# Experts: routing weights spread over partitions by DMA, expert weights laid out by the host, a quarter of the tokens routed first

## What is computed

```python
logits = x @ gate_w.T;  scores = sigmoid(logits);  sc = scores + e_bias
group_scores = top_k(sc.reshape(T, 8, 4), 2)[0].sum(-1)
masked = where(group in top_k(group_scores, 4), sc, 0)
topk_idx = top_k(masked, 6)[1];  topk_w = scores at topk_idx, normed, * 2.5
combine = zeros(T, 32) with topk_w at topk_idx
h = relu(einsum('th,eih->tei', x, up_w)) ** 2 * combine[:, :, None]
out = einsum('tei,ehi->th', h, down_w) + relu(x @ shared_up_w.T) ** 2 @ shared_down_w.T
```

## Time and profile before

| what | us |
|---|---|
| median of 3 runs (3858.93 to 3862.2) | 3859.53 |
| the profiled execution | 3866.06 |
| its span, first to last instruction | 3864.3 |
| PE busy in the span | 3442.3 (89%) |
| DVE busy | 2871.3 (74%) |
| ACT busy | 2329.9 (60%) |
| POOL busy | 1067.8 (28%) |

### The profile page before, as it was taken

One profiled execution on the slowest core, in us unless ns is written; L12 is line 12 of the kernel. 1 busy time (PEld: TensorE's weight loads), 2 busy tenths in 40 slices (PEclk: granted clock), 3 DMA queues, 4 the chain that ended last, 5 costly groups with the idle time before them and its releaser, 6 DMA issues. The chain is left out here.

```text
span 3864.3 us, 97882 instructions
## 1 busy us (share of the span) xinstructions
PE 3442.3 (89%) x39003; PEld 1703.8 (44%) x39003; DVE 2871.3 (74%) x3920; ACT 2329.9 (60%) x4575; POOL 1067.8 (28%) x1874
## 2 busy tenths in 40 slices
PE   5885999999999999984999582999999999999988
PEld 3442444444444444433666581444444444444435
DVE  5776788888888888854344896888888888888852
ACT  3663677777777777771332530777777777777663
POOL 4552223222222322201665002232222223222201
PEclk9997999999999999996999795999999999999998
DMA  3332222232222223201000002222322222232200
GB/s 98 75 79 58 61 55 60 55 77 61 56 63 54 59 58 75 57 12 25 1 0 1 0 0 61 53 60 56 76 63 54 63 54 59 62 70 63 49 16 22
DMA packets 165138, 194.88 MB, mean 50 GB/s; under 512 B 32166, under 2 KB 124123, under 8 KB 164715
## 3 DMA queue, kind: packets, MB, share of 16 engines
q1 hardware_dynamic: 164714, 189.03, 20.8%
HBM read 27.88 MB, written 2.10 MB: 8 GB/s over the span
## 5 line engine op out<-in xcount | busy, mean ns | idle before, releaser
L586 ACT ACTIVATE cross_Pr<-cross_sT 128x512 f32<-128x512 f32 (+1 forms) x3584 | 1833.6, 563 | 768.8 <-PE cross_sT L508 767.8
L649 DVE TENSOR_REDUCE cross_nm<-cross_ring 128x2 f32<-128x802 f32 x2048 | 1975.6, 991 | 323.7 <-PE cross_ring L474 295.3
L508 PE MATMUL cross_sT<-cross_Q,cross_K 64*128 64x256 bf16 x13312 | 1044.2, 273 | 49.3 <-ACT cross_Pr L586 42.2
L527 PE MATMUL cross_oT<-cross_Pr,cross_V 128*9 128x256 f32 x13312 | 1029.8, 381 | 0.0
L508 PEld LDWEIGHTS cross_sT<-cross_Q,cross_K 64*128 64x128 bf16 x13312 | 511.1, 95 | 771.8 <-ACT cross_Pr L586 637.1
L474 PE MATMUL cross_ring<-cross_K,cross_Q 64*128 64x401 bf16 x4096 | 662.3, 337 | 62.2 <-DMA cross_K<-cross_kparts 33.5
L401 POOL TENSOR_TENSOR cross_mp<-cross_nm,cross_one 128x8 bf16<-128x8 f32 x128 | 25.9, 202 | 1373.6 <-DVE cross_nm L654 1373.6
L527 PEld LDWEIGHTS cross_oT<-cross_Pr,cross_V 128*9 128x9 f32 x13312 | 197.6, 88 | 412.6 <-issue 245.1
L474 PEld LDWEIGHTS cross_ring<-cross_K,cross_Q 64*128 64x128 bf16 x4096 | 199.0, 94 | 202.7 <-DVE cross_nm L649 106.9
L1104 DVE TENSOR_TENSOR moe_rc<-moe_r,moe_bank 128x512 f32<-128x512 f32 x128 | 87.9, 687 | 170.8 <-ACT moe_r L995 170.8
L876 POOL TENSOR_TENSOR moe_hh<-moe_r,moe_rc 128x512 f32<-128x512 f32 x128 | 162.5, 1270 | 160.0 <-DVE moe_rc L1104 159.3
(11 more groups left out here) (296 smaller groups left out, 3035.7 us busy)
## 6 DMA issues: line engine op xcount, KB each, us to landing
cross_K<-cross_kparts SPq DMA_DIRECT2D x1152, 100.1 KB, 2.3
cross_in<-in_ctx_T_dram SPq DMA_DIRECT2D x32, 600.4 KB, 5.5
self_QK<-self_parts SPq DMA_DIRECT2D x144, 128.0 KB, 2.7
cross_Q<-cross_qparts SPq DMA_DIRECT2D x288, 64.0 KB, 2.1
X<-in_x_dram SPq DMA_DIRECT2D x4, 512.0 KB, 6.1
self_in<-in_x_T_dram SPq DMA_DIRECT2D x16, 128.0 KB, 2.3
cross_Q<-cross_mst SPq DMA_DIRECT2D x128, 16.0 KB, 1.8
out_dram<-X SPq DMA_DIRECT2D x1, 2048.0 KB, 8.7
```

The source lines that it names most:

```text
L508: mm = pe.matmul(sT[0:r, cfg.sT_bank(b, u + j), (c % 2) * S:(c % 2 + 1) * S], K[ROWS * j:ROWS * (j + 1), pair, t, s:s + r], Q[ROWS * j:ROW ...
L527: mm = pe.matmul(oT[32 * j:32 * j + VR, 0:S], V[0:r, b % VB, c, 4 * g + j, :], Pr[0:r, slot, (c % 2) * S:(c % 2 + 1) * S], start=(c == 0), ...
L586: act.activation(Pr[0:r, u % NPR, 0:nc_ * S], sT[0:r, cfg.sT_bank(b, u), 0:nc_ * S], ACT.Exp).then_inc(exped, 1)
L649: dve.tensor_reduce(nm4[:, g % 2, t, :, pk, blk], R.rearrange("p (j n) -> p j n", j=2)[:, :, 0:cfg.block], AX.X, ALU.max, negate=True).the ...
```

## The change

Eight things change, all in experts and in what the host hands over.

1. The host lays out the gate, up and down weights as PE needs them (`moe_gate`, `moe_up`, `moe_down`). The transposes of weights on PE and their copies go away. Gate, up and down have a semaphore each, and the first transposes of X wait for no load.
2. The spread product on PE (sel by cT) goes away, with sel, the split into three bf16 parts, and banks 2 and 3 for it. cT is now f32, 32 partitions x 4096.
3. In its place SP issues one DMA for each of the 128 routed chunks. It reads two neighbouring partitions of cT, each 64 times over, and writes the 128 partitions of a buffer crep in rows of 2048 bytes (256 KB). There are eight buffers, and one is issued again when DVE has used it.
4. DVE multiplies r by crep, both in SBUF.
5. Token tiles 0 to 7 are scored and routed first; the routing of the other 24 is a generator of 28 pieces, of which DVE does one after each chunk of the loop. PE transposes the routing weights of 8 tiles at a time, ahead of chunks 4, 34, 46 and 66.
6. In each block the two shared chunks come first.
7. Up products use banks 0 to 3, and PE runs three chunks ahead; r, rc and hh are four deep; outputs alternate between banks 4 and 5.
8. All loops are written out, none is a hardware loop.

```diff
-            sp.dma_start(raw_gate[:, :], a["L0_ffn_gate_w"]).then_inc(loaded, 16)
...
+            sp.dma_start(gate[:, :], a["moe_gate"]).then_inc(gate_in, 16)
+            sp.dma_start(ebias[:, :], a["L0_ffn_e_bias"].partition_broadcast(P)).then_inc(gate_in, 16)
+            sp.dma_start(up[:, :, :].rearrange("p m n -> p (m n)"), a["moe_up"]).then_inc(up_in, 16)
+            sp.dma_start(down[:, :, :].rearrange("p m n -> p (m n)"), a["moe_down"]).then_inc(down_in, 16)
+            for n in range(TOTAL):
+                i, m, q = chunk(n)
+                if q is None:
+                    continue
+                if m == 0:
+                    sp.wait_ge(c_took, i * BT // GROUP + 1)
+                if q >= SPREADS:
+                    sp.wait_ge(scaled, q - SPREADS + 1)
+                src = cT[2 * m:2 * m + 2, i * BLK:(i + 1) * BLK].unsqueeze(1).broadcast_to([2, MI, BLK])
+                sp.dma_start(crep[:, q % SPREADS, :], src).then_inc(crep_in[q % SPREADS], 16)
...
-                if m < NC:
-                    if not first:
-                        pe.wait_ge(scaled, i * NC + m - 1)
-                    pe.matmul(bank[:, 2 + m % 2, :], sel[:, m, :], cb, start=True, stop=True)\
-                      .then_inc(spread, 1)
...
+            for u in range(GROUP // BT):
+                turn_x(u)
+            pe.wait_ge(gate_in, 16 * 2)
+            score(0)
+            for u in range(GROUP // BT, NBLK):
+                turn_x(u)
+            score(1)
+            pe.wait_ge(took, NBLK)
+            pe.wait_ge(up_in, 16)
+            pe.wait_ge(sig, 2)
+            for n in range(TOTAL + LEAD):
+                if n in TURN_AT:
+                    turn_c(TURN_AT[n])
+                if n < TOTAL:
+                    rise(n)
+                if n == LEAD:
+                    pe.wait_ge(down_in, 16)
+                if n >= LEAD:
+                    fall(n - LEAD)
...
-                    dve.tensor_tensor(rc[:, m % 3, :], r[:, m % 3, :], bank[:, 2 + m % 2, :], ALU.mult)\
+            for n in range(TOTAL):
+                i, m, q = chunk(n)
+                if q is not None:
+                    dve.wait_ge(relu, n + 1)
+                    if n >= BUFS:
+                        dve.wait_ge(hidden, n - BUFS + 1)
+                    dve.wait_ge(crep_in[q % SPREADS], 16 * (q // SPREADS + 1))
+                    dve.tensor_tensor(rc[:, n % BUFS, :], r[:, n % BUFS, :], crep[:, q % SPREADS, :], ALU.mult)\
                        .then_inc(scaled, 1)
...
+                next(later, None)
+                if i > 0 and m == 3:
+                    residual(i - 1)
+                if i > 0 and m in (4, 5, 7):
+                    norm(i - 1, {4: (0,), 5: (1,), 7: (2,)}[m])
```

More of the change, by code:

```diff
@@ L809, in experts @@
         block = ctx.enter_context(nc.Block())
[L811 to L834, removed]
+        per = 1 + 3 * BT
@@ L899, in _ @@
                 mm.then_inc(turned, 1)
[L900 to L913, removed]
@@ L941, in output, with score @@
[L941 to L944, removed]
+            def score(part):
+                lo, hi = PARTS_OF[part]
+                pe.wait_ge(took, hi // BT)
+                for t in range(lo, hi):
+                    mm = pe.matmul(logit_bank(part)[:, (t - lo) * NE:(t - lo + 1) * NE], xT[:, t * P:(t + 1) * P],
+                                   gate[:, :], start=True, stop=True)
+                mm.then_inc(logits, 1)
@@ L945, in output, with fall @@
+            def fall(n):
+                i, m, q = chunk(n)
+                first, last = n % NCH == 0, n % NCH == NCH - 1
+                if first and i >= 2:
+                    pe.wait_ge(ln_dve, (i - 2) * per + 1)
+                pe.wait_ge(hidden, n + 1)
                 for t in range(BT):
-                    mm = pe.matmul(bank[:, 4, t * D:(t + 1) * D], hh[:, m % 3, t * P:(t + 1) * P], down[:, m, :],
-                                   start=(m == 0 and t == 0), stop=(m == NCH - 1), skip_group_check=True)
@@ L948, in output @@
-                if m == NCH - 1:
+                    mm = pe.matmul(bank[:, 4 + i % 2, t * D:(t + 1) * D], hh[:, n % BUFS, t * P:(t + 1) * P],
+                                   down[:, m, :], start=(first and t == 0), stop=last, skip_group_check=True)
+                if last:
                     mm.then_inc(summed, 1)
-            def block_of(i, has_next):
-                for m in range(NCH):
-                    if m + 2 < NCH:
-                        up_and_spread(i, m + 2)
-                    elif has_next:
-                        up_and_spread(i + 1, m + 2 - NCH)
-                    output(i, m)
@@ L997, in _, with sigmoids @@
-            rectify(0)
-            with act.Fori(1, NBLK) as i:
-                rectify(i)
-        steps = [0]
+            def sigmoids(part):
+                lo, hi = PARTS_OF[part]
+                act.wait_ge(logits, part + 1)
+                act.activation(s0[:, lo:hi, :].rearrange("p t e -> p (t e)"), logit_bank(part)[:, 0:(hi - lo) * NE],
+                               ACT.Sigmoid).then_inc(sig, 1)
+            for u in range(NBLK):
+                act.wait_ge(turned, u + 1)
+                act.activation(xT[:, u * BLK:(u + 1) * BLK], bank[:, u % 4, :], ACT.Copy).then_inc(took, 1)
+                if u == GROUP // BT - 1:
+                    sigmoids(0)
@@ L1003, in _ @@
         @block.vector
         def _(dve):
+            steps = [0]
             def link(ins):
```

356 lines of the change are left out of this document (155 added, 201 removed).

## The result

The changed kernel took 4534.05 us (median of 4 runs, 4530.90 to 4534.99) against 3859.55 before (4 runs): a ratio of 1.1744, 95% interval 1.1727 to 1.1762, or 674.5 us more. The direction and the cause were as predicted, and the time lies in the range; the forecast of 4750 was 216 us too long.

What follows compares the result with a forecast made beforehand. PE's products bound the loop, a chain the preparation; spread DMAs would then set the pace. First spread near 1770 plus 128 x 9.5 = 1216 and the tail ends at 2996, +887 us: 4750, range 4180 to 4900.

Steps and rivals of the forecast that it cites:

- I take 9.5 us: Routed loop, spread by DMA: two neighbouring source rows draw on one group's 27.7 GB/s, so each spread takes 9.5 us.
- rival 1: Spread by DMA: two rows each read at an engine's best rate, 5.8 us a spread, 4273 us in all; chance 0.31.
- the forecast's own 9 to 10.5: Spread by DMA: a group's rate sets some 9 to 10.5 us a spread, 4750 us in all; chance 0.50.
- The number of engines: Spread by DMA: an outermost dimension of 2 gives two engines; by this or by shared ports, DMAs set the pace.
- Rival 4: Spread by DMA: each source partition is the limit, 6.9 GB/s, 18.9 us a spread, 5950 us in all; chance 0.05.
- Rival 2: Spread by DMA: the DMAs keep up, at most 1.76 us a spread; 77 us saved, 3783 us; chance 0.08.
- Rival 3: Routed loop: DMAs keep up but DVE and POOL take turns, 1.96 us a chunk; 24 us saved, 3836; chance 0.06.
- The preparation: Before the loop: PE starts at 1739.4, routing of 8 tiles takes DVE 12 us, first spread near 1770.
- The 49 us of the earlier start: Before the loop: the first routed chunk could be fed near 1770 instead of 1819, 49 us earlier.
- The loop's 28 us: Routed loop: the spread product leaves PE, 128 x 0.22 = 28 us saved.
- the 77: Experts' stage: 49 us of earlier start and 28 us of loop, 77 us saved if everything else keeps PE's pace.
- The end and the signs: Experts' stage: 10 us behind the last spread; signs: stage 1250 us, crep wait 7.5, traffic 28 GB/s, landing after 75 us.

## Why the prediction was right, and by what it was off

**The spread's pace: right in kind, mis-sized.** The step "I take 9.5 us", with its 128 x 9.5 = 1216 us, is the one that was off. From the first issue at 1766.0 to the last scaling at 2768.1 there are 1002 us, 7.83 for a spread: 214 us less, of the 216 by which the forecast missed. The reasoning under it held: neighbours share a limit of a group of four rows. In step (first gaps of 10.5 us on average), two rows of a group give 262 / 10.5 = 25 GB/s, against the 27.7 worked out from the stacking. What was missing is that eight spreads are in flight, and that the two engines need not be at the same one. Once apart they draw on two groups for every other spread, and those take 5.1 us, which is rival 1's pace (51 GB/s in the kernel with rows 16 apart, where 45 was worked out). The truth is the forecast's mechanism in the first gaps, and at the end one spread by it and one at rival 1's pace by turns. So 7.83 us lies between the forecast's own 9 to 10.5 and rival 1's 5.1 to 5.8, in neither. By the prediction's sum, 9 to 10.5 us alone would have given an estimate of 4680 to 4880; the time lies in the range because the range took in both mechanisms, of which the run had a mixture that nobody had forecast. That is in part luck.

The Trainium skill ("SBUF — State Buffer", section "Door 1: The DMA port swizzle") puts partitions 0 to 3, 4 to 7 and so on in groups on one port each, two groups that lie 32 apart on the same one, and gives 27.2 GB/s a port. The runs here agree, at 25.5 GB/s rather than 27.2: 25 GB/s for two rows in one group, 51 for two in different ones, and sharing by fours in the rhythm. By the page's table eight rows 16 apart lie on four ports, 109 GB/s; the kernel with eight source rows falls back to about 103 again and again. Its mean of 119 in the window shown is over that because of the peaks of up to 167, which by the account above (not tested in this kernel) are stretches in which engines at two spreads reach more ports.

**The number of engines: no part in the time.** The claim that either limit alone would set the pace was not needed. The share of 0.12 shows two engines for an outermost dimension of 2, and with all 16 taken the time was the same, 4560 against 4534.

**Rival 4, each partition its own limit: fallen.** One row alone gives 25.5 GB/s, not 6.9.

**Rival 2, the DMAs keep up: fallen for two rows, true for sixteen.** There DVE waits for one spread only.

**Rival 3, turns of DVE and POOL: real, hidden in the change, and priced too high.** It was put at 53 us. Taking it away, with the DMAs out of the way, gave 18.4 us (3827.4 to 3809.0). The pitch of 1.89 against PE's 1.75 holds only in stretches; the shared chunks and the buffers between them let PE stay busy for 146.8 of 150 us (1850 to 2000) in the sixteen-row kernel. With the change as it is, scalings take 692 ns, since POOL is seldom at work beside them.

**The preparation: right.** The routing of eight tiles ran from 1745.72 to 1758.7, 13 us where 12 were worked out; the first spread was issued at 1766.01, 4 us ahead of the predicted 1770. The 49 us of the earlier start stand beside the 51.1 of the kernel with the product back on PE, which has the early start, the written-out loops and the order of chunks, but no DMA. Its chunks keep the 1.97 us of before, so the start is the gain. PE began at 1737.5, without the wait for all loads, as foreseen. That this is 1.9 us ahead of the predicted 1739.4 is no part of the change: the layer before ended 1.9 us earlier in that execution (its last step on DVE began at 1736.59, before at 1738.52), and in the kernel with eight spreads, the same on PE up to there, PE began at 1739.58.

**The loop's 28 us: right, with a price beside them.** With bf16 copies and the scaling from PSUM the whole gain is 65.2 us of the 77. An estimate of the rest from the rows: 16 x 0.22 = 3.5 us of copies and 12 to 13 for the first spread, if PE has nothing to do meanwhile. That makes 51 + 28 - 16 = 63. No run takes these two prices away one by one.

**The end and the signs.** From the last scaling to the end 8.8 us, predicted 10. The stage took 1039 us where 1250 were expected, the wait for crep was 849.6 / 126 = 6.7 us where 7.5 were, and the traffic 27 GB/s and then 36 to 37 where 28 was, all by the same step. The landing time of 75 us is not in the page; an estimate by SP's wait for the scaling eight back is about eight gaps, 62 us on average. One sign failed by itself: PE was to be busy for less than a quarter of the loop, and was for 40 and 48% of it. The prediction had the clock fall but did not count that PE's work then takes longer: at 2407.45 us, in a window at clock 0.51, the eight products of an output took 2.08 us, against 1.05 in the loop before. PE waits for POOL all the same, so this costs next to nothing.

## What to carry to other kernels

A broadcast out of a few SBUF rows is priced by where those rows lie and not by its bytes: count the groups of four partitions it reads from, including those of the transfers in flight with it, at some 25 GB/s each. Groups can share even so: eight rows 16 apart had the rate of four groups, not eight. Compare GB/s with the need before moving work from an engine to a DMA. Here 0.22 us of PE a chunk was exchanged for 7.8 us of DMA. With the source in 16 places the DMAs are hidden, and yet that kernel took 3827 us where the product back on PE took 3809; scaling from PSUM made the two equal, and only with bf16 copies as well did the exchange win, by 13 to 14 us (3796). Look then for what the new operand does: an input moved from PSUM to SBUF can put two engines into turns that no single duration shows. And price the parts of a change separately, since the larger of the two gains here (51 of 65 us) needed no DMA at all.

## What the runs showed of the hardware that was not expected

- Two DMA engines that start in step on one group of rows seem to drift apart: gaps of 10.4 and 10.8 us at first, 5.1 and about 9.2 by turns some 400 us later, with traffic at 25 or 50 GB/s and little between. With an order of chunks that lets them part for good, it took some 140 us. Why they drift, and why faster in one order, was not tried.
- Eight source rows 16 apart, read by eight engines, fall back to about 103 GB/s, four times the 25.5 of one group, though they lie in eight groups of four.
- 16 engines at a busy share of 0.87 moved 33 GB/s. A DMA share near full is no sign of bandwidth; share and GB/s have to be read together.
- A DVE instruction with two SBUF inputs that begins beside POOL's product ended 0.54 to 0.56 us after it in the rows shown, whatever its start; with one input in PSUM it takes its own 0.69 us.
